# Weighting expert outputs in the copy out of PSUM and adding them in memory by the scatter

## The reference

```python
x = L0_attn_x                                   # (2, 1024, 256)
h = _layernorm(x) * (1 + ca) + sa
x = x + ga * attention(h)                       # 16 heads of 16, causal
h = _layernorm(x) * (1 + cb) + sb
cw = _combine_weights(h, gate_w)                # (2048, 16), 4 of them not zero, of 2 groups of 4 experts
out = 0
for e in range(16):
    out = out + cw[:, e:e+1] * (_swiglu(h @ expert_up_w[e].T) @ expert_down_w[e].T)   # 176 features
out = out + _swiglu(h @ shared_up_w.T) @ shared_down_w.T                              # 352 features
x = x + gb * out
```

## Time and profile before

| | |
|---|---|
| median of 3 runs | 633.51 us |
| the profiled execution: its time, its span | 636.28 us, 634.5 us |
| PE, DVE, ACT, POOL busy | 92%, 75%, 61%, 51% of the span |
| HBM read, written | 60.70 MB, 43.65 MB |

### The profile page before, as it was taken

One profiled execution on the slowest core, in us unless ns is written; L12 is line 12 of the kernel. 1 busy time (PEld: TensorE's weight loads), 2 busy tenths in 40 slices (PEclk: granted clock), 3 DMA queues, 4 the chain that ended last, 5 costly groups with the idle time before them and its releaser, 6 DMA issues.

```text
span 634.5 us, 13733 instructions
## 1 busy us (share of the span) xinstructions
PE 586.5 (92%) x3977; PEld 401.8 (63%) x3977; DVE 474.4 (75%) x1394; ACT 387.3 (61%) x941; POOL 324.4 (51%) x571
## 2 busy tenths in 40 slices
PE   4997899999999999998899697898899999999996
PEld 4885534443444434453333286787799999999985
DVE  4968988888888777778846667778776666776648
ACT  4764576666676655656758354264466777776662
POOL 4115553747475636836467877572144444444430
PEclk9989999999999999988968798899899999999999
DMA  8289669846265662653014143577954444444498
GB/s 294 77 207 248 169 159 270 181 127 144 101 132 184 156 200 65 124 202 119 2 65 175 48 176 121 220 225 277 356 177 134 132 136 136 137 132 133 121 381 337
DMA packets 67234, 107.56 MB, mean 170 GB/s; under 512 B 13641, under 2 KB 52313, under 8 KB 66010
## 3 DMA queue, kind: packets, MB, share of 16 engines
q1 hardware_dynamic: 60298, 87.67, 47.5%
q0 software_dynamic: 6864, 19.01, 7.7%
HBM read 60.70 MB, written 43.65 MB: 164 GB/s over the span
## 4 chain that ended last, share of the span: by engine, by line
PE 66%; DVE 16%; POOL 7%; DMA 5%; issue 4%; SPq 1%; ACT 1%; DVEq 0%; ACTq 0%; POOLq 0%
PE bank L2499 11%; PE bank L2240 9%; PE bank L2254 8%; PE bank L2141 8%; POOL chosen_rows L1191 5%; DVE mxB L1576 4%; DVE mxA L1576 3%; PE bank L2168 3%; PE bank L2139 3%; PE bank L2453 3%; PE bank L2511 2%; DMA Z<-expert_rows 2%; PE bank L2408 2%; PE bank L2197 1%; PE bank L2523 1%
## 5 line engine op out<-in xcount | busy, mean ns | idle before, releaser
L1438 ACT ACTIVATE Pr<-bank 128x512 f32<-128x512 f32 (+3 forms) x384 | 166.1, 495 | 101.7 <-PE bank L2254 97.2
L1257 POOL DMA_INDIRECT expert_rows<-Y,YIX x79 | 75.8, 959 | 105.3 <-DVE ytmp L2014 76.8
L1576 DVE TENSOR_REDUCE mxA<-bank 128x1 f32<-128x128 f32 (+3 forms) x256 | 112.2, 484 | 21.1 <-PE bank L2141 20.9
L2254 PE MATMUL bank<-Qs,Ks 99*128 99x512 bf16 (+3 forms) x384 | 120.7, 341 | 3.3 <-ACT Pr L1438 2.7
L2141 PE MATMUL bank<-Ks,Qs 96*128 96x512 bf16 (+3 forms) x384 | 120.0, 330 | 1.3 <-DVE mxB L1576 0.6
L1576 DVE TENSOR_REDUCE mxB<-bank 128x1 f32<-128x512 f32 x128 | 81.6, 682 | 12.9 <-PE bank L2141 12.8
L2240 PE MATMUL bank<-Pr,Vst 128*32 128x512 f32 (+3 forms) x768 | 86.4, 524 | 4.4 <-POOL Pr L1241 4.4
L1239 POOL TENSOR_TENSOR tick<-ident 128x1 f32<-128x1 f32 x128 | 26.6, 208 | 106.5 <-ACT Pr L1438 105.5
L1191 POOL DMA_INDIRECT chosen_rows<-Hx,pos x64 | 66.9, 1046 | 25.2 <-issue 18.6
L2499 PE MATMUL bank<-W,xh 128*128 x316 | 78.6, 330 | 0.6 <-issue 0.6
L2254 PEld LDWEIGHTS bank<-Qs,Ks 99*128 99x128 bf16 x384 | 36.4, 100 | 58.6 <-ACT Pr L1438 39.0
(11 more groups left out here) (256 smaller groups left out, 1300.3 us busy)
## 6 DMA issues: line engine op xcount, KB each, us to landing
G<-chosen_rows SPq DMA_DIRECT2D x79, 132.0 KB
Z<-expert_rows SPq DMA_DIRECT2D x16, 512.0 KB, 11.3
W<-expert_words SPq DMA_DIRECT2D x7, 1088.0 KB, 7.2
qk_parts<-AP SPq DMA_DIRECT2D x32, 192.0 KB, 3.1
Wraw<-in_wexp SPq DMA_DIRECT2D x9, 608.0 KB, 4.9
SA<-in_wexp SPq DMA_DIRECT2D x7, 608.0 KB, 5.1
Vst<-Vall SPq DMA_DIRECT2D x8, 512.0 KB, 5.8
expert_words<-SH SPq DMA_DIRECT2D x7, 480.0 KB, 3.6
```

The costliest lines, as they stand in the source:

```text
L1257: nc.gpsimd.indirect_dma_start(out=zd, out_offset=bass.IndirectOffsetOnAxis(ap=YIX[:, b:b + 1], axis=0), in_=Y[b % YRING], in_offset=None) ...
L1438: nc.scalar.activation(Pr[(2 * s + j // 2) % 4][:, j % 2, 0:w], ebank[p % RING][:, 0:w], ACT.Exp, scale=SCALE).then_inc(exp_done, EXP)
L1576: nc.vector.tensor_reduce(dst, mbank[u % RING][:, 0:w], AX.X, ALU.max).then_inc(m_red, 1)
L2254: nc.tensor.matmul(ebank[p % RING][:, 0:CH - q0], Ks[slot][0:NAUG, j, kt * P:(kt + 1) * P], Qs[slot][0:NAUG, qc, j, q0:CH], start=True, st ...
```

## The change

Each token's four outputs are no longer stored apart and summed at the end. They are weighted when they leave PSUM, and the scatter adds them to rows in memory.

- **The row's extra data** (META 8 to 12) now also hold the four weights. The target of an output is row t of sum 0 or row t of sum 1: the chosen experts of a token are ranked by number, ranks 0 and 2 go to sum 0, ranks 1 and 3 to sum 1 (nine router steps behind the choice instead of four behind the places; POOL's copy of `TQ` into the rows is gone).
- **ACT's copy** multiplies by the weight, a scale for each partition. The 40 diagonal matrices and the 24 scalings are gone.
- **The scatter** has `compute_op=ALU.add`. Two blocks in flight together may not hold one target row, so the scatter of block b waits until that of b - 2 has landed. Its row numbers are converted by a POOL instruction in front of it.
- **The sums are zeroed** by four DMAs in attention's items 1 to 4 (4.3 MB).
- **Eleven row buffers** instead of four: eight of them lie on the shared expert's weights, so the load of block 3 waits until the shared expert is done.
- **The end**: sum 0 is loaded when blocks of experts 0 to 14 have landed, sum 1 when all have: 4 MB in 8 DMAs. PE adds the two for five pairs with the identity as weights, 12 products; DVE does two pairs and POOL one, with three operations each.

```diff
-META = 2 * TOPK
+META = 3 * TOPK
...
-ZROWS = T * TOPK + (NE + SPARE) * P
+SUMS = 2
+ZROWS = SUMS * (T + P)
...
-GRING, YRING = 4, 4
+GRING, GLATE, YRING = 11, 3, 4
+IWRING = 16
+ZERO_DMAS = 4
+ZERO_AT = (1, 2, 3, 4)
...
-PE_PAIRS, DVE_PAIRS = (0, 2, 4, 6, 7), (1, 3, 5)
+PE_PAIRS, DVE_PAIRS, POOL_PAIRS = (0, 2, 4, 6, 7), (1, 5), (3,)
...
+            def zero_sums(i):
+
+                lo, hi = (j * (ZROWS // P) // ZERO_DMAS for j in (i, i + 1))
+                sp.dma_start(zd.rearrange("(p n) h -> p n h", n=ZROWS // P)[:, lo:hi, :],
+                             PADZ[:, :].unsqueeze(1).broadcast_to([P, hi - lo, H])).then_inc(zeros_out, 16)
...
                     sp.wait_ge(t1_ps, b - GRING + 1)
                     sp.wait_ge(yix_step, 2 * (b - GRING) + 2)
-
+                if b == GLATE:
+
+                    sp.wait_ge(s_down, 2 * NC)
...
-            for t in range(NT):
-                load_outputs(sp, t)
+            for r in range(SUMS):
+                least = MIN_NEEDED if r == SUMS - 1 else NE - SUMS + 1 + r
+                sends = [...]
+                for i in range(YRING):
+                    sp.wait_ge(y_sc[i], sends[i])
+                for i in range(Z_PARTS):
+                    load_outputs(sp, r, i)
...
             def scatter_block(b):
 
-                pool.wait_ge(y_read, b + 1)
                 pool.wait_ge(yix_step, 2 * b + 2)
+                nc.gpsimd.tensor_copy(YIX[:, b:b + 1], IW[:, b % IWRING, 0:1]).then_inc(yix_made, 1)
+                pool.wait_ge(y_read, b + 1)
+                pool.wait_ge(yix_made, b + 1)
+                if b == 0:
+                    pool.wait_ge(zeros_out, 16 * ZERO_DMAS)
+                if b >= SUMS:
+
+                    pool.wait_ge(y_sc[(b - SUMS) % YRING], 16 * ((b - SUMS) // YRING + 1))
                 nc.gpsimd.indirect_dma_start(
                     out=zd, out_offset=bass.IndirectOffsetOnAxis(ap=YIX[:, b:b + 1], axis=0),
-                    in_=Y[b % YRING], in_offset=None).then_inc(y_sc[b % YRING], 16)
+                    in_=Y[b % YRING], in_offset=None, compute_op=ALU.add).then_inc(y_sc[b % YRING], 16)
...
-                nc.scalar.activation(Y[u % YRING], ybank[:, 0:H], ACT.Copy).then_inc(y_read, 1)
+                act.wait_ge(yix_step, 2 * u + 2)
+                nc.scalar.activation(Y[u % YRING], ybank[:, 0:H], ACT.Identity, scale=IW[:, u % IWRING, 1:2]).then_inc(y_read, 1)
...
             def find_outputs(b):
 
                 g, tmp = G[b % GRING], ytmp[b % 2]
-                nc.vector.scalar_tensor_tensor(out=tmp[:, :], in0=g[:, H:H + TOPK], scalar=EBR[:, b:b + 1],
-                                               in1=g[:, H + TOPK:ROWW], op0=ALU.is_equal, op1=ALU.mult).then_inc(yix_step, 1)
+                nc.vector.scalar_tensor_tensor(out=tmp[:, :, :], in0=g[:, H:H + TOPK].unsqueeze(1).broadcast_to([P, 2, TOPK]),
+                                               scalar=EBR[:, b:b + 1], in1=g[:, H + TOPK:ROWW].rearrange("p (a j) -> p a j", j=TOPK),
+                                               op0=ALU.is_equal, op1=ALU.mult).then_inc(yix_step, 1)
...
-            def add_outputs(i, u):
+            def add_outputs(i, u, n):
 
                 t = 2 * PE_PAIRS[i] + u
-                pe.wait_ge(z_in[t], z_count(t))
-                pe.wait_ge(diag_done, TOPK * (2 * i + u + 1))
-                for j in range(TOPK):
-                    ins = nc.tensor.matmul(sums_of(i, u, 1)[:, 0, :], DG[:, 2 * i + u, j, :], Z[:, t, j, :],
-                                           start=(j == 0), stop=(j == TOPK - 1))
+                for r in range(SUMS):
+                    ins = nc.tensor.matmul(allb[i + u][:, 0:n * H], ident[:, :],
+                                           Z[:, r, t:t + n, :].rearrange("p t h -> p (t h)"), start=(r == 0), stop=(r == SUMS - 1))
                 ins.then_inc(z_ps, 1)
```

More of the change, by code:

```diff
@@ L223 @@
 }
+SEL_DONE, PLACED, POS_DONE, ROUTE_STEPS = 24, 33, 35, 35
 UNIT_DVE = {
@@ L324 @@
 COUNT_AT = 8
[L327 removed]
+PE_PAIRS, DVE_PAIRS, POOL_PAIRS = (0, 2, 4, 6, 7), (1, 5), (3,)
 LAST_PAIR = NT // 2 - 1
[L329 to L334, removed]
+assert LAST_PAIR in PE_PAIRS and sorted(PE_PAIRS + DVE_PAIRS + POOL_PAIRS) == list(range(NT // 2))
+ADD_STEPS = 3
+Z_PARTS = 4
 SP_LOAD, SP_AHEAD = 4, 6
[L338 removed]
+TOT_STEPS, COUNT_STEPS, N_FCONST, PADS_MADE = 13, 4, 11, 5
 def program(nc, x, wqk, bqk, wv, bv, wout, bout, cT, wmod, wgate, wsh, wexp, qkd, modrows, hTd, xd, padd, zd, wd, out):
@@ L386, in program @@
         Hx0 = rows.put("Hx0", [P, TPC, ROWW], F32)
-        TQ = rows.put("TQ", [P, NT, TOPK], F32)
+        TQ = rows.put("TQ", [P, NT], F32)
         EBR = rows.put("EBR", [P, NB], F32)
@@ L390, in program @@
         YIX = rows.put("YIX", [P, NB], U32)
-        W4 = rows.put("W4", [P, NT, TOPK], F32)
+        IW = rows.put("IW", [P, IWRING, 2], F32)
         RK = rows.put("RK", [P, TPC, TOPK], F32)
@@ L396, in program @@
         rbt = rows.put("rbt", [1, NB + 1], I32)
-        ytmp = [rows.put(f"ytmp{i}", [P, TOPK], F32) for i in range(2)]
+        ytmp = [rows.put(f"ytmp{i}", [P, 2, TOPK], F32) for i in range(2)]
         att0 = BASE + KEEP + ROWSZ
@@ L472, in program @@
         CBr = under.put("CBr", [P, B, H], F32)
[L473 to L477, removed]
+        PADZ = under.put("PADZ", [P, H], F32)
+        Z = nc.alloc_sbuf_tensor_at("Z", [P, SUMS, NT, H], F32, offset=att0 + NSH * EW * 4)
+        assert NSH * EW + SUMS * NT * H <= PLACE[NW - 1] * EW
         late = Area(att0 + NW * EW * 4, early0 + EARLY - att0 - NW * EW * 4)
@@ L485, in program @@
             SH.append(nc.alloc_sbuf_tensor_at(f"SH{i}", [P, RAW], F32R, offset=PRE_AT + (2 * i + 1) * RAW * 4))
-        G = [late.put(f"G{i}", [P, ROWW], F32) for i in range(GRING)]
+        GROW = -(-ROWW * 4 // 32) * 32
+        assert (GRING - GLATE) * GROW <= EW * 4
+        G = [late.put(f"G{i}", [P, ROWW], F32) if i < GLATE else
+             nc.alloc_sbuf_tensor_at(f"G{i}", [P, ROWW], F32, offset=att0 + (i - GLATE) * GROW) for i in range(GRING)]
         xh = [late.put(f"xh{i}", [P, H], F32R) for i in range(2)]
```

163 lines of the change are left out of this document (89 added, 74 removed).

## The result

The change makes the kernel slower. Four runs gave a median of 688.27 us (682.98 to 689.85), against 633.55 (633.21 to 636.86) for the kernel before on the same chip: a ratio of 1.082, interval [1.077, 1.088]. The forecast was 626.9 with a range of 622 to 650.

A forecast was written before the change was run, and what follows sets the result against it. PE was taken to bound the block loop and DMA the end. A gain of 6.9 us at the end less 0.3 lost at the start gave -6.6 on the median 633.51: 626.9 us, range 622 to 650.

The forecast's parts named there:

- Part 2: Block loop: PE keeps its 2.02 us a block, POOL's 1.6 us hides, and the added wait costs nothing in quiet stretches.
- The tick row: Block loop: the profile row from which POOL's conversion of one column was priced at 0.21 us.
- L: Block loop: time from a scatter's start to its landing, taken as 3.1 us with the addition, bounds 2.37 and 5.1.
- threshold: Block loop: the landing time, 3.96 us, past which the wait for the scatter two back would set the pace.
- The rule (L + 0.08) / 2: Block loop: pace in us a block set by the wait for the scatter two back, 0.08 from landing to waiter.
- the add is slow and the scatter sets the pace: Rival, block loop: at L = 4.4 a pace of 2.24 us, +17 us, 644 in all; chance 0.28.
- Part 3: Start of the block loop: block 3's load waits for the shared expert, 0.3 us lost, up to 2.8 later.
- Part 1: End of the program: both sums loaded before PE is through, DMA leaves the path, gain 6.9 us.
- the second rival: Block loop's start and end: crowded scatters and row loads give the gain back, 630 to 634 us; chance 0.13.
- Part 4: Zeroing in attention and added router steps: nothing, up to 1 us for the router, 3 us a piece if zeroing's cover failed.

The follow-up runs named there:

- e12: The kernel before with the adding scatter on zeroed rows and the conversion on POOL, no wait for a landing: 673.64 us, ratio 1.067.
- e2: The changed kernel with plain scatters, the addition in memory left out, waits and conversions kept: 643.48 us, ratio 1.017.
- e3: The kernel before with POOL converting the row numbers ahead of each plain scatter: 634.24 us, ratio 1.001.
- e4: The kernel before with scatters that add on rows zeroed beforehand, no wait for a landing: 637.78 us, ratio 1.005.
- e11: e4 with the wait for the scatter two back added, no conversion on POOL: 668.92 us, ratio 1.057.
- e9: The kernel before with SP's load of block 3's rows waiting for the shared expert: 640.05 us, ratio 1.009.
- e1: The changed kernel with the conversion of row numbers moved from POOL to DVE: 671.76 us, ratio 1.058.
- e6: e1 with eight Y buffers instead of four: 671.83 us, ratio 1.059.
- e10: e2 with both sums loaded only after block 71 has landed: 645.32 us, ratio 1.021.
- e5: e1 with both sums loaded only after block 71 has landed: 672.44 us, ratio 1.062.
- e8: e1 with three sums, so a scatter waits for the one three back and 6 MB are loaded at the end: 649.40 us, ratio 1.025.

## Why the prediction was wrong, point by point

**The step that failed is Part 2**, "POOL's work is 1.26 + 0.21 + about 0.15 for the dependent wait = 1.6 of 2.02 us. It hides". It is 2.50 (e12). Term by term:
- The row: 1.57 instead of 0.96. The text named this ("should its row grow from 0.96 by over 0.4") but gave it no price beside the landing's; it had itself listed "POOL might write twice the descriptors, 0.96 more", and then added that only to L, never to POOL's list. It is three times the packets, and 0.6 us of POOL's time.
- The conversion: its row shows 0.78 instead of 0.21. The tick row was taken in attention, with no scatter under way. Behind a plain scatter 0.20 holds (e2, e3). Here it starts 0.99 us into a row of 1.57 and ends 0.20 behind that row's end, so what it adds to the list is still 0.20; the rest of the 0.78 is the scatter's row a second time.
- The gap: 0.73 instead of 0.30 + 0.15. So 1.57 + 0.20 + 0.73 = 2.50, where the text had 0.96 + 0.21 + 0.45 = 1.62: the row is 0.61 over, the gap 0.28. The trace of before had a row for it that was not read, a router scatter behind a POOL copy:
```profile
384.27 0.98 POOL L1191 DMA_INDIRECT chosen_rows<-Hx,pos  x1 [0.78 <-POOL Hx L1186]
385.56 0.96 POOL L1191 DMA_INDIRECT chosen_rows<-Hx,pos  x1 [0.30 <-issue]
```
  An indirect DMA that waits for the instruction ahead of it starts 0.78 behind that one's end; the earlier trace rows showed only the case with nothing to wait for.

With the longer gap and a plain scatter the list is 0.98 + 0.20 + 0.75 = 1.93 (e2) and hides; it is the addition that takes it over 2.02.

**L and its threshold, Part 2 again.** L was taken at 3.1 and is 3.8 to 4.1. The rule (L + 0.08) / 2 had its 0.08 from SP's queue; POOL's scatter takes 0.76, so the threshold was not 3.96 but 2 x 2.02 - 0.76 = 3.28. The forecast's own L lay 0.2 under that, and the measured one is over it. The rival "the add is slow and the scatter sets the pace", 0.28, is what happened, in both its forms; its price of 17 us (644) was too low even for the landing alone, +31 over e4 in e11, and the two are not additive: two blocks of the list take 5.0 us, which covers a median landing's 4.1 + 0.76, so on top of the list only the longer landings show. The 70 steps are 7.1 us longer after than in e12, and that ahead of block 71 is 5.2 longer. The Trainium skill ("DMA: Bandwidth & Descriptors", Anatomy of one DMA) was read as speaking for a full further trip of 1.41; the rows lie between none and that: behind its row a scatter that adds takes 3.8 - 1.57 = 2.2 to 4.1 - 1.57 = 2.5 us, 0.8 to 1.1 more than the plain 1.41.

**Part 3, the start.** Taken at 0.3, bounded by 2.8. By the stretch behind the shared expert e9 gives 2.7 against before, and the kernels with the wait lie 1.9 to 4.9 over those without; e9's median says 6.3. That is at the bound or over it. The sum counted bytes "in full" from 445.4, as if SP issued them without a hole. Weights 13 had been under way since 441.07 in time that was free; held back behind the wait, they leave the DMA engines at a quarter for 4 us and then stand in front of block 4's rows. The slow rows behind that, at a granted clock of 0.50, are part of it.

**Part 1, the end.** The mechanism held: PE's sums start at 668.14 without waiting for Z, right behind its last product for the spare blocks, DMA is off the path. The sizes did not. From block 71's scatter, forecast and after: until PE's sums 12.4 and 14.7 (spare blocks beside the loads, with scatters at 2.50), until DVE starts 1.9 and 3.1 (PE's granted clock was 0.69 there), DVE 11.9 and 14.6 (three additions beside POOL's take 5.6 instead of 2.1), the last store 2.3 and 2.2: 28.5 and 34.7. In e2, with the plain scatter, they are 14.2, 2.9, 13.8 and 2.6. POOL's pair was put at "nothing", which was right for its own end (680.95, DVE's is 685.87) and wrong for DVE's. The crowding of the second rival is real: landings of 7 to 11 us beside the Z loads (7.4, 7.7 and 9.5 after, 10.8 in e1). The forecast had "about one us of it" show at the end, since four Y buffers let ACT run on. What binds is the scatter's own wait for the one two back, which no Y buffer bridges (e6): the step ahead of block 71 is 5.2 us over 2.50, and two behind it 1.3 and 2.1. In the kernels without that wait (before, e3, e4, e9, e12) no step is over 3.6 us. When the loads start later, the gaps come later (e10, in part e5).

**Part 4** (zeroing, router) is not seen on its own. e2 has everything but the addition, at 10 us by the medians over before and 5.5 by the spans: 2.7 behind the shared expert and 4.9 in the 70 steps, one of them 4.2 us beside the Z loads, less 1.8 at the end and 0.5 ahead of it all. What the nine router steps and the zeroing cost was not tried apart. The shared expert is done at 443.3 to 447.9 us in the kernels with both and at 442.3 to 446.5 in the others, so a cost of an us or two would not be seen. What also stays open is how far the removal of 4 MB of loads could be turned into a gain at all: none of the versions tried, the best at 649.4 with the addition, reaches the kernel before.

## What to carry to other kernels

Before giving an engine a dependent instruction in a loop, add up its list with rows taken in the same company: a small operation behind a DMA-issuing one, and a DMA that waits, cost other than either alone. A wait has a price on the engine that waits, so the latency from an event to the start of the waiter must be read on that engine, not on another's queue. And two changes that are free one at a time can share one slack: e3 and e4 each fitted into POOL's idle 1.06 us a block, together they went 0.5 over it. Last, more buffers ahead of an instruction do not help while that instruction itself waits for a landing (e6).

## What the runs showed of the hardware that was not expected

- An indirect DMA of 128 rows of 1 KB that adds in memory: 1.57 us on POOL, 3.6 at the least and 3.8 to 4.1 in the median to land, some 1.1 to 1.2 us of each DMA engine and 144 packets; a plain one 0.96, 2.4, 0.34 and 48.
- A conversion of one column on POOL: 0.20 us behind a plain indirect DMA, 0.78 behind one that adds. An addition of 128x512 there: 1.28 (e2) and 1.85. Each starts some 1.0 us into the adding DMA's row and ends as if it had begun at that row's end: 0.99 + 0.78 = 1.57 + 0.20, and 1.01 + 1.85 = 2.86 against 1.56 + 1.28 = 2.84.
- From the landing of a scatter to the start of POOL's indirect DMA that waits for it: 0.76 us; SP's load starts 0.08 behind.
- Additions of 128x512 on DVE beside POOL's: 2.82, 1.04 and 1.75 us instead of 0.69. They end at 678.16, 679.84 and 681.51, each some 0.55 us behind the end of one of POOL's three (677.60, 679.29, 680.95). DVE's product at 678.09, with one input from PSUM, took 0.68 beside POOL's second.
- With the DMA engines at 0.85 of the loop (e4, e8), PE and the row loads lost nothing measurable; loads of several MB in a burst stretch landings to 7 to 11 us, and scatters that wait for a landing then start 4 to 10 us apart; without such a wait no two are over 3.6 us apart (e4, e12).
